# Masks of the attention scores laid in PSUM by ScalarE, before TensorE adds the scores on top

## The reference

```python
xn = layernorm(x)                                   # over the last axis
q, k, v = split(xn @ w_qkv + b_qkv)                 # 16 heads of 16
# heads 0..3 are global, heads 4..15 are local
gmask = (i - j) < 0
lmask = ((i - j) < 0) | ((i - j) > 64)
scores = where(mask, -inf, q @ k.T * 16 ** -0.5)
ctx = softmax(scores) @ v
x + ctx @ w_out + b_out + ffn(xn)
```

## Time and profile before

| | us |
|---|---|
| median of 3 runs (1655.19 to 1657.1) | 1655.23 |
| the profiled execution | 1654.62 |
| its span, first to last instruction | 1652.9 |
| TensorE busy | 1563.5 (95%) |
| VectorE busy | 937.7 (57%) |
| ScalarE busy | 684.4 (41%) |
| GpSimd busy | 284.2 (17%) |

### The profile page before, as it was taken

The page is one execution under the profiler, slowest core; times in us unless marked ns, Lnnn a source line. Parts: engine busy times, 40 slices in busy tenths (PEclk is TensorE's granted clock), DMA queues, the critical chain, the costliest instruction groups (busy, mean ns, idle before and its releaser), DMA issues.

```text
span 1652.9 us, 36914 instructions
## 1 busy us (share of the span) xinstructions
PE 1563.5 (95%) x15489; PEld 1112.8 (67%) x15489; DVE 937.7 (57%) x2048; ACT 684.4 (41%) x1224; POOL 284.2 (17%) x346
## 2 busy tenths in 40 slices
PE   5899999999999999999999999999999999999997
PEld 4576675767757676676757767576675767667674
DVE  6665672737537484564837567274763748447461
ACT  3426245261543517243362523626254351634425
POOL 2011121211112111121201212021111201112111
PEclk9999999999999999999999999999999999999999
DMA  8514417072350906218071350806326080530800
GB/s 207 63 31 88 80 34 123 10 117 51 76 89 4 151 15 104 61 38 130 4 122 45 77 91 21 125 21 106 62 64 100 4 139 27 96 69 23 132 4 14
DMA packets 128186, 116.48 MB, mean 70 GB/s; under 512 B 19251, under 2 KB 127668, under 8 KB 127972
## 3 DMA queue, kind: packets, MB, share of 16 engines
q1 hardware_dynamic: 128020, 114.12, 38.5%
HBM read 73.43 MB, written 34.34 MB: 65 GB/s over the span
## 4 chain that ended last, share of the span: by engine, by line
PE 76%; DVE 14%; ACT 5%; issue 4%; POOL 1%; DMA 0%; DVEq 0%; ACTq 0%; POOLq 0%
PE PS L587 33%; PE PS L714 8%; DVE block_peak L1204 4%; PE PS L793 3%; PE PS L825 3%; PE PS L732 3%; PE PS L856 3%; PE PS L766 3%; PE PS L807 3%; PE PS L772 3%; DVE prod L1273 2%; PE PS L726 2%; DVE prod L1276 2%; ACT HE L1029 2%; PE PS L746 2%
## 5 line engine op out<-in xcount | busy, mean ns | idle before, releaser
L1446 POOL TENSOR_TENSOR PL<-prod,PH 128x512 fp32r<-128x512 f32 x128 | 164.5, 1285 | 792.7 <-ACT PH L1003 792.7
L1003 ACT ACTIVATE PH<-prod 128x512 fp32r<-128x512 f32 x128 | 80.8, 631 | 428.8 <-DVE prod L1276 428.8
L587 PE MATMUL PS<-XH,WH 128*128 128x512 f32 x512 | 220.4, 430 | 4.5 <-DVE XL L1145 1.9
L587 PE MATMUL PS<-XH,WL 128*128 128x512 f32 x512 | 203.6, 398 | 0.0
L587 PE MATMUL PS<-XL,WH 128*128 128x512 f32 x512 | 203.2, 397 | 0.0
L1204 DVE TENSOR_REDUCE block_peak<-PS 128x4 f32<-128x512 f32 x288 | 186.9, 684 | 4.2 <-PE PS L746 4.2
L993 ACT ACTIVATE prod<-PS 128x512 f32<-128x512 f32 x128 | 76.3, 596 | 231.3 <-PE PS L587 220.3
L1029 ACT ACTIVATE HE<-PS 128x512 f32<-128x512 f32 (+1 forms) x320 | 159.7, 552 | 26.1 <-PE PS L807 23.5
L1197 DVE TENSOR_REDUCE peak<-PS 128x4 f32<-128x512 f32 x192 | 125.6, 685 | 41.0 <-PE PS L732 41.0
L1273 DVE TENSOR_TENSOR prod<-PS,prod 128x512 f32<-128x512 f32 x128 | 88.1, 689 | 104.6 <-PE PS L701 104.6
L714 PE MATMUL PS<-UH,PH 128*128 128x256 f32 x512 | 139.5, 306 | 0.0
(11 more groups left out here) (195 smaller groups left out, 3154.8 us busy)
## 6 DMA issues: line engine op xcount, KB each, us to landing
parts_d<-area SPq DMA_DIRECT2D x32, 768.0 KB, 5.1
area<-parts_d SPq DMA_DIRECT2D x128, 192.0 KB, 12.4
area<-parts_d SPq DMA_DIRECT2D x32, 576.0 KB, 12.5
tok<-in_L_attn_x_dram SPq DMA_DIRECT2D x16, 512.0 KB, 6.5
xt<-in_L_attn_x_dram SPq DMA_DIRECT2D x16, 512.0 KB, 3.9
out_dram<-xt SPq DMA_DIRECT2D x16, 512.0 KB, 3.7
area<-parts_d SPq DMA_DIRECT2D x96, 64.0 KB, 5.9
Vs<-Va SPq DMA_DIRECT2D x24, 204.0 KB, 7.6
```

Of the source, the lines that this page charges most:

```text
L587: ins = e.matmul(ps, a, b, start=first and k == 0, stop=last and k == n - 1, skip_group_check=True)
L1003: e.activation(PH[:, h, :], prod[:, j % 3, :], ACT.Copy).then_inc(phi)
L1446: e.tensor_tensor(PL[:, j % 2, :], prod[:, j % 3, :], PH[:, j % 2, :].bitcast(F32), ALU.subtract).then_inc(plo)
```

## The change

On ScalarE, a stage `seed` copies the mask tile (bf16, repeated by its access pattern) into the PSUM bank, `ACT.Copy`, 128x512. The TensorE stage of a bank that was laid this way waits for the count `seeded`, leaves out the mask product and lets the small products add onto what lies in the bank. The bank is claimed for the later stage at the point of the plan where the seed stands (`claim`), and the seed waits for the last reader of the stage before in that bank.

What is laid: the local peaks of a chunk except the first three, the diagonal global peaks, and the local scores except the first two of a chunk. The others keep the mask product. A peak's seed stands in the plan right behind the peak two before it; a score's seed right behind the score two before it. For the first diagonal peak of an odd chunk that is ahead of the `rows` of the local peaks.

```diff
-    def add_lpeak(ch, t, grp):
-        add_on("lpeak", ch, t, grp, uses=[peak_use()])
+    def add_lpeak(ch, t, grp, bank):
+        add_scores(("lpeak", ch, t, grp), [bank])
 ...
+    def add_scores(stage, uses):
+
+        bank, *slots = uses
+        laid = stage in where
+        if laid:
+            add(*stage, uses=slots)
+        else:
+            add(*stage, uses=uses)
+            where[stage] = [int(bank[-1])]
+        where[stage] += [int(u[-1]) for u in slots]
+
+    def add_seed(bank, *stage):
+
+
+        add("seed", *stage)
+        plan.claim(stage, [bank])
+        where[stage] = [int(bank[-1])]
 ...
@@ def local_groups(ch):
         units = [(grp, half) for grp in range(1, 1 + NL // 4) for half in range(2)]
+        scores = [(ch, grp, half, pair, score_use()) for grp, half in units for pair in range(2)]
         order = []
         for n, (grp, half) in enumerate(units):
-            order.append([(add_lscore, ch, grp, half, pair) for pair in range(2)])
+            order.append([])
+            for m in (2 * n, 2 * n + 1):
+                order[-1].append((add_lscore, *scores[m]))
+                if m + 2 < len(scores):
+                    order[-1].append((add_seed, scores[m + 2][4], "lscore", *scores[m + 2][:4]))
 ...
@@ def peak_groups(ch):
-        order = [[(add_lpeak, ch, t, grp)] for t in range(T) for grp in range(NL // 4)]
+        order = [[(add_lpeak, ch, t, grp, peak_use())] for t in range(T) for grp in range(NL // 4)]
+        gpeaks = [[(add_gpeak, ch, t, j, peak_use())] for t in range(T) for j in range(c * T + t + 1)]
+        for n, ((stage, *key),) in enumerate(order + gpeaks):
+            if stage is add_lpeak and n > 2:
+                order[n - 2].append((add_seed, key[-1], "lpeak", *key[:-1]))
+            elif stage is add_gpeak and key[2] == c * T + key[1]:
+                (order + gpeaks)[n - 2].append((add_seed, key[-1], "gpeak", *key[:-1]))
         order[-1].append((add, "found", ch, 0))
-        gpeaks = [[(add_gpeak, ch, t, j)] for t in range(T) for j in range(c * T + t + 1)]
         gpeaks[2].append((add_rows, ch, 0))
 ...
@@ TensorE, lpeak
-                    take(i, *stage)
-                    e.matmul(psum(i).rearrange("p (a k) -> p a k", a=4), ident_b[:, :],
-                             peak_mask_l[:, which, :].unsqueeze(1).to_broadcast([P, 4, P]), start=True, stop=False, skip_group_check=True)
+                    if stage in laid:
+                        q.wait_ge(seeded, nth("seed", *stage))
+                    else:
+                        take(i, *stage)
+                        e.matmul(psum(i).rearrange("p (a k) -> p a k", a=4), ident_b[:, :], local_peak_mask(ch, t),
+                                 start=True, stop=False, skip_group_check=True)
 ...
@@ TensorE, gpeak
-                    take(i, *stage)
                     if diag:
-                        e.matmul(psum(i).rearrange("p (a k) -> p a k", a=4), ident_b[:, :], peak_mask_g[:, :].unsqueeze(1).to_broadcast([P, 4, P]),
-                                 start=True, stop=False, skip_group_check=True)
+                        q.wait_ge(seeded, nth("seed", *stage))
+                    else:
+                        take(i, *stage)
 ...
@@ TensorE, lscore
-                    take(i, *stage)
-                    e.matmul(psum(i).rearrange("p (w q) -> p w q", w=8), ident_b[:, :],
-                             mask_l[:, :].unsqueeze(1).to_broadcast([P, 8, WINDOW]), start=True, stop=False, skip_group_check=True)
+                    if stage in laid:
+                        q.wait_ge(seeded, nth("seed", *stage))
+                    else:
+                        take(i, *stage)
+                        e.matmul(psum(i).rearrange("p (w q) -> p w q", w=8), ident_b[:, :],
+                                 mask_l[:, :].unsqueeze(1).to_broadcast([P, 8, WINDOW]), start=True, stop=False, skip_group_check=True)
 ...
@@ ScalarE
+                elif kind == "seed":
+                    of, i = key, bank_of(*key)
+                    take = bank_read[i], use(f"bank{i}", *of) - 1
+                    if of[0] == "lpeak":
+                        q.wait_ge(*take)
+                        e.activation(psum(i).rearrange("p (a k) -> p a k", a=4), local_peak_mask(*of[1:3]), ACT.Copy).then_inc(seeded)
 ...
+                    else:
+                        q.wait_ge(*take)
+                        e.activation(psum(i).rearrange("p (w q) -> p w q", w=8), mask_l[:, :].unsqueeze(1).to_broadcast([P, 8, WINDOW]),
+                                     ACT.Copy).then_inc(seeded)
```

## The result

| | before | after |
|---|---|---|
| median, us (20 runs each) | 1655.19 (1653.01 to 1657.1) | 1657.95 (1652.87 to 1660.35) |
| ratio | | 1.0016, 95% interval 1.0008 to 1.0023 |
| span of the profiled execution | 1652.9 | 1658.1 |
| mean granted clock of TensorE | 0.996 | 0.984 |

The account below looks back on a forecast made before the run. TensorE was taken to bound the kernel, busy 95% of the span, with VectorE taking turns in odd peaks. A pair sums -2.82 + 0.80 + 0.70 + 0.21 = -1.11 us, times eight -8.9: 1646 us, range 1628 to 1666.

Parts of the forecast that it names:

- Even peaks: Peaks of an even chunk: masks removed from TensorE outweigh one returning stall, 2.82 us saved per pair of chunks.
- Local scores: Copies chained between exponentials on ScalarE delay the scores: +0.80 us in an even chunk, +0.21 in an odd one.
- Odd peaks: Peaks of an odd chunk: copies queued on ScalarE delay TensorE and VectorE, +0.70 us at the end.
- the products of the second diagonal block: Odd chunk's peaks: their copy queues behind a high-part copy waiting for VectorE, so they start 0.47 us later.
- those of the third: Odd chunk's peaks: the third diagonal block waits for a later VectorE reduce plus a copy, +0.84 us.
- signs of being wrong: Copies under 0.5 or over 0.7 us, even chunks saving under 1 us, or odd-peak stalls much over 0.9 us.
- rival D: New TensorE idle gaps halve its clock in a local stretch, costing up to 26.6 us, 1673 or more; chance 0.03.
- (a): Odd peaks: copies for peaks 4 and 5 queue behind the high-part copy; peak 5's products begin at 972.53, not 971.93.
- (b): Odd peaks: first diagonal copy waits for VectorE's reduce, holding the peak-rows copy; weight row starts at 987.92, 986.81 before.
- Rival A: Everywhere: masks vanish from TensorE and ScalarE keeps ahead; pair -7.7, kernel -62 us, 1593; chance 0.07.
- C: Whole kernel: gains and stalls cancel within 0.2%, even peaks saving 2 us in place of 2.8; chance 0.15.
- B: Local scores: dearer ScalarE chain links make it slower; gain gone at 0.14 us per link, 1663 at 0.27; chance 0.20.

Follow-up runs that it names:

- e4: Changed kernel with only the local-score copies kept, all peak masks back on TensorE; 1668.23 us, ratio 1.0086.
- e10: Changed kernel with both long TensorE gaps of odd chunks, before local peak 4 and before the weight row, filled by repeated products; 1645.56 us, ratio 0.9941.
- e8: e4 with ScalarE's order changed: both exponentials of a pair first, then both copies; 1658.66 us, ratio 1.0026.
- e3: Changed kernel with the local scores' masks all back on TensorE, peak copies kept; 1644.33 us, ratio 0.994.
- e1: Changed kernel with the gap before local peak 4 of odd chunks filled by making the bank-opening product four times; 1650.06 us, ratio 0.9974.
- e2: Changed kernel with local peaks 4 and 5 of odd chunks masked by TensorE again; 1644.38 us, ratio 0.9946.
- e7: e2 with the peak-rows stage put ahead of the first diagonal copy in odd chunks; 1637.08 us, ratio 0.9891.
- e6: Kernel before plus copies at even chunks' local and diagonal peaks and odd chunks' local peaks 3 and 6 to 11; 1617.7 us, ratio 0.9776.

## Why the prediction was wrong

The forecast was a gain of 9 us; the result is a loss of 2.8. The terms, each per chunk or pair:

- **Even peaks, -2.82.** Measured -3.45: from the first mask of chunk 8 to the first local score's products it was 42.93 us (874.72 to 917.65) and is 39.48 (878.20 to 917.68). The direction and the cause were right, the size was not: I let the small products of two peaks in a row take 0.69 us without masks, and they take 0.57, and I had kept 0.19 back. TensorE's rows of the changed kernel show it (start to start, 981.74 to 982.31):

```profile
981.74 0.64 PE L772 MATMUL PS<-area 96*64 96x128 bf16 x16
982.31 0.39 PE L752 MATMUL PS<-UH,PH 128*128 128x256 f32 x1
```

- **Local scores, +0.80 and +0.21.** Measured +1.21 and +0.86 (e4). The chain was right: the wait for the own last instruction costs 0.03 us, as taken (918.12 + 0.60 to 918.75), and score 3 began 1.04 us later against 0.99 walked. Mis-sized was the instruction behind a copy: it starts 0.53 us after the copy's start (918.75 to 919.28), not 0.48 as between exponentials. That is a term that I should have bounded, since it comes in every link. With it the first product of the next chunk behind score 7, walked at +1.58, stands at +1.72 (926.80 where 925.05 was, less the 0.03 by which the first products of the stretch are apart). And the late copy at scores 10 and 11, walked at 0.14, costs 0.31: from their start to the next product it is 0.79 us (933.50 to 934.29) against 0.92 with both masks (932.18 to 933.10), so 0.13 is saved of 0.44. These two are 0.3 of the 0.41 that I missed in an even chunk. In e4's chunk 9 score 7 is late by 1.35 and the last pair costs the same 0.3; my +0.21 had no such walk written down, and why it is 0.65 short I can't lay to one step. (By its own terms, 1.58 - 0.88 + 0.14, the even figure would have been 0.84.)
- **Odd peaks, +0.70.** Measured without the clock's fall, in e10: from the first mask of chunk 9 to the first local score's mask it is 48.24 us (957.97 to 1006.21) against 47.74 before (965.41 to 1013.15), so +0.50. The stalls came at their places and near their sizes: counted from that first mask, the weight row is 0.99 late (walked 1.11), the products of the second diagonal block 0.37 (0.47), those of the third 0.78 (0.84). What I never wrote down is how long TensorE stands idle in them: in the changed kernel 1.40 us before peak 4 and 1.81 before the weight row, though a stall much longer than 0.9 us at a place was one of my own signs of being wrong.
- **The clock, at nothing.** This is the step that failed. The sum has no term for the granted clock; it stood only in rival D, at a chance of 0.03, in a local-score stretch, priced at that stretch's length, 26.6 us. It happened in the peaks of odd chunks, behind the gaps of 1.40 and 1.81 us that my steps (a) and (b) make, nine times in seven odd chunks and a tenth time in chunk 15, at 1.34 us or a little more each. Between the changed kernel and e10, which has no fall ahead of chunk 15's scores, lie 12.4 us, more than the whole gain. My evidence against it was the clock at 1.00 in three windows, beside an idle time of 0.73 us. The trace of before held better evidence, which I did not look at: in chunk 15 it has a gap of 1.66 us, and the clock is at 1.2 GHz from 1.7 us behind it. TensorE is half idle in between (0.85 of 1.70 us busy), so it is not quite the case of the new gaps, but it is a fall beside a gap of their length. Row and windows of the kernel before:

```profile
1601.31 0.39 PE L766 MATMUL PS<-mask_l,ident_b 128*128 128x512 bf16 x1 [1.66 <-DVE block_peak L1204]
1601.30:1603.00 1.70, 0.85 (x13) 0.59 (x13) 1.20 (x5) 0.60 (x1) 0.77 (x1) 1.00 0.00 0
1603.40:1606.20 2.80, 2.80 (x51) 2.22 (x50) 0.00 (x0) 1.59 (x3) 0.00 (x0) 0.50 0.03 9
```

So without the falls the pair comes to -2.24 + 1.40 = -0.84 us where I had -1.11, from terms that missed in both directions: 0.6 too little gain at the even peaks, 1.06 too little loss at the scores, 0.2 too much loss at the odd peaks. That e10 ends at 1645.56, beside my 1646, is therefore partly luck; eight such pairs are 6.7 us, and 1.4 more come from an earlier first opening product (82.31 against 83.71 us). The range held nothing against the result (1658 lies within 1628 to 1666), but the sign was wrong. Rival A did not occur. The time fell where C had put it, inside 0.2%, but not by C's mechanism, since the even peaks saved more than I took and not less. B's mechanism, the chain of ScalarE, is real (e8): the wait per link is the 0.03 that I had taken, with 0.05 on top for the instruction behind a copy, far from the 0.14 of B. B's own figures do not come out: with 64 links the gain of 8.9 is gone at x = 0.17, not 0.14, and 0.2% slower is reached at 0.22, not 0.19.

## What to carry to other kernels

Take work off the bounding engine only where the engine that gets it is ahead at that point: a helper's in-order queue decides instruction by instruction, and here 256 moves brought 53 us and the 112 others, with the stalls and the falls of the clock that they made, took all of it back. When a sum makes new idle gaps on TensorE, write down their length, look in the whole trace of before for gaps as long and at the granted clock behind them, price that as a term of its own, and test it by filling the gap with repeated products. Before an extra instruction is put into a queue, look at who stands behind it: one copy ahead of the peak rows cost 7 us.

## What the hardware showed

- Behind a gap of 1.40 us (peak 4) on TensorE a granted clock of 0.50 followed in four of seven odd chunks of the changed kernel and in five of seven of e3; behind one of 1.80 us (weight row) in five of seven of the changed kernel, five of seven of e1, four of seven of e2 and six of seven of e3. It lasted about 3.4 us each time, even where TensorE was fully busy again (3.00 of 3.00 us in 974 to 977). Gaps of 0.4 to 0.96 us, as at the local scores, and the seven of 1.07 us in e7 were not followed by one; one of 1.21 us in chunk 15's peaks was followed by one in e1 and by none in e6. What decides between them stays open.
- A copy from SBUF to PSUM of 128x512 takes 0.59 to 0.60 us on ScalarE, as long as one from PSUM to SBUF (0.596). The Trainium skill (ScalarE: Activation LUTs, The pipeline for one element) says that ScalarE writes faster to PSUM than to SBUF; against the copy SBUF to SBUF (0.63) the trace agrees, by 0.03 us, though that one reads float32 and this one bf16.
- On ScalarE, the instruction behind a mask copy starts 0.53 us after the copy does, against 0.48 us behind an exponential. The two differ in source and in target. The copy of the high part, SBUF to SBUF, is followed after 0.54 us (972.15 to 972.69), so the time goes with reading SBUF rather than with writing PSUM, as far as these three forms tell.
